# A gated cross-attention block with routed experts: rows stored, next slot numbers and row quarters issued ahead of the w1 load, the w1 split ahead of the row transposes, and another order at the seam

## The chip, the cores and the metric

The kernel runs on one core of one Trainium2 chip. The metric is the device time in microseconds (us) of one execution. A core has five engines with a queue each: TensorE (PE) multiplies matrices, VectorE (DVE), ScalarE (ACT) and GpSimd (POOL) do elementwise work, SyncE (SP) starts transfers. An instruction starts when those before it on its engine have gone ahead and the semaphores it waits for have been raised.

## The reference

The input x is 16 batches of 256 tokens with 512 features, the context as large. All is float32.

```python
x = x + tanh(g_xattn) * softmax((ln(x) @ Wq) @ (ctx @ Wk).T / sqrt(512)) @ (ctx @ Wv)
n = ln(x)                                      # layer norm again
probs = softmax(n @ gate_w + gate_b, axis=1)   # over the tokens of a batch, 8 experts
vals, idx = top_k(probs, 2)
h = relu(n @ w1[e] + b1[e]); h = relu(h @ w2[e] + b2[e]); y = relu(h @ w3[e] + b3[e])
v[e] = sum of y * w_tok over all tokens that chose expert e
x = x + tanh(g_ffn) * (sum of v[e] over the two experts of a token)
```

## The kernel before

Each float32 product is done as three products of parts: an operand is split into a rounded part (`_hi`, a copy by ACT or DVE) and the rest (`_lo`, a subtraction by DVE or POOL), and PE adds hi*hi, hi*lo and lo*hi (`split_product`, L1319 to L1321).

**First part: batches.** For each of the 16 batches the attention, the second norm and the gate are computed, the two best experts of every token are found (`two_best`), PE ranks them (`ranks`), and DVE gives every chosen token a slot in its expert's region (`slots`). POOL writes pairs of token and weight to these slots in DRAM (`send_pairs`, `slot_pair`). The normed rows go to DRAM (`xn2_dram`).

**Second part: tiles.** The slots of an expert are cut into tiles of 352. There are 24 tiles here. For a tile, the slot numbers are loaded (`load_idx`), POOL gathers the rows with three indirect transfers (`gather`, L664), and the rows are brought into feature order. For tiles 0 to 3 PE transposes them (`row_transposes`). From tile 4 on SP stores the gathered rows to `rows_dram` (`store_rows`), loads them back as four quarters (`load_quarters`, `xq`), and DVE transposes 32x32 blocks (`transpose_blocks`, L1195). ACT and DVE split the result (`et_high`, `et_low`). Then come three layers: 48 matmuls of 352 columns each (two halves of 24), with ReLU by ACT (`relu`, L836), the `_hi` cast by DVE (`h_high`, L1190) and the `_lo` subtraction by POOL (`h_low`, L674) in two halves each between them. The weights w1, w2, w3 of the tile's expert are loaded if the expert changed (`load_w`), rounded by ACT (`split_w`, L825) and subtracted by DVE (`w_low`, L930). DVE sums the third layer's result over the tile with the tokens' weights (`weighted_sum`, L1221), and `part_done` is raised.

**The order is written out by hand, one list for each engine.** In the loop, iteration j:
- PE: layer 2 of tile j, layer 1 of tile j+1, layer 3 of tile j. Layer 1 of tile m waits for `part_done` of tile m-2, layer 3 for both halves of POOL's `h_low` of layer 2.
- ACT: w3 round of j, ReLUs of layer 2 of j, w2 round of j+1, ReLUs of layer 1 of j+1, w1 round of j+2, `et_high` of j+2. The w1 round of j+2 waits until layer 1 of j+1 is through, since there is one `w_hi` and one `w_lo` for each layer.
- DVE: w3 split of j, `h_high` of layer 2 of j, w2 split of j+1, `h_high` of layer 1 of j+1, row transposes of j+2, w1 split of j+2, `et_low` of j+2, weighted sum of j.
- POOL: `h_low` of layer 2 of j, of layer 1 of j+1, gather of j+3.
- SP: w3 and b2 of j+1, w2 and b1 of j+2, w1 of j+3, rows store of j+3, b3 and token weights of j+1, quarters of j+3, slot numbers of j+4.

A load of w1 is four transfers, a rows store two, the quarters four, the slot numbers three. SP waits in order: for the w1 load that DVE has split the w1 before; for the store and for the slot numbers that the gather has landed; for the quarters that the store has landed and that the transposes before are done; for b3 and the token weights that the tile before is summed.

**The seam** is the stretch in which the last batches and the first tiles are interleaved, on each engine a list of its own between the batch pipeline and the loop (from L1238 on DVE, from L1553 on PE, from L856 on ACT).

Of the kernel before, what the change touches and what calls it, by code (L numbers as in the profile page):

```python
# [15 lines left out]
P = 128  # L16
B, S, D, E = 16, 256, 512, 8
TOK = B * S
TOPK = 2
DC = D // P  # L20
# [72 lines left out]
def has_tile(ahead, left):  # L93

    return ahead < left


def flamingo_block(nc, x, x_t, ctx_t, g_xattn, g_ffn, wq_t, wk_t, wv, gate_w, gate_b,
# [15 lines left out]
    with ExitStack() as ctx:  # L114
# [287 lines left out]
        def _(sp):  # L402
# [140 lines left out]
            def tile(j, left):  # L543
                if has_tile(1, left):
                    load_w(2, j + 1)
                    load_b(1, j + 1)
                if has_tile(2, left):
                    load_w(1, j + 2)
                    load_b(0, j + 2)
                if has_tile(3, left):  # L550
                    load_w(0, j + 3)
                    if not isinstance(j, int):
                        store_rows(j + 3)
                if has_tile(1, left):
                    load_b(2, j + 1)
                    load_wb(j + 1)
                if has_tile(3, left) and not isinstance(j, int):
                    load_quarters(j + 3)
                if has_tile(4, left):
                    load_idx(j + 4)  # L560

            tile(0, AHEAD + 1)
            tile(1, AHEAD + 1)
# [153 lines left out]
        def _(act):  # L717
# [123 lines left out]
                relu_half(n, m, 0)  # L841
                relu_half(n, m, 1)

            def et_high(m):
                need(act, l_done[0], 2 * m)
                if not isinstance(m, int):
                    act.wait_ge(et_ready, m - BY_BLOCKS + 1)
                    act.activation(et_hi[:], et[:], ACT.Copy).then_inc(et_his, TH)
                    return
                for c, (a, n) in enumerate(CHUNKS):  # L850
                    act.wait_ge(te_done, TH * m + c + 1)
                    act.activation(et_hi[:, :, a:a + n], row_banks(m)[c][:, 0:DC * n].rearrange("p (c s) -> p c s", c=DC),
                                   ACT.Copy).then_inc(et_his, 1)
# [4 lines left out]
            v_high(B - 1)  # L858
            pt_high(B - 1)
            gt_high(B - 2)  # L860
            et_high(0)
            split_w(0, 0)
            gate_exp(B - 2)
            split_w(1, 0)
            act.wait_ge(b_in[0], 16)
            relu_half(0, 0, 0)
            norm2(B - 1)
            relu_half(0, 0, 1)
            et_high(1)
            gt_high(B - 1)  # L870
            split_w(0, 1)
# [32 lines left out]
        def _(dve):  # L904
# [276 lines left out]
                dve.wait_ge(w_his[n], m + 1)  # L1181
                low(w_lo[n][:], w_raw[n][:], w_hi[n][:], w_los[n])

            def h_high(n, m):
                need(dve, l_done[n + 1], 2 * m)
                if n == 1 and isinstance(m, int) and m == 0:
                    dve.wait_ge(gate_done, B)
                for k in range(2):
                    dve.wait_ge(relu_done[n], DC * m + 2 * k + 2)
                    dve.tensor_copy(h_hi[n][:, 2 * k:2 * k + 2], h[:, 2 * k:2 * k + 2]).then_inc(h_his[n], 1)  # L1190

# [3 lines left out]
                dve.transpose(et[:].rearrange("p k (g b) -> p g k b", b=QB),  # L1195
                              xq[:].rearrange("p g (i k) -> p g k i", k=DC)).then_inc(et_ready, 1)

            def et_low(m):
                if not isinstance(m, int):
                    dve.wait_ge(et_his, TH * (m + 1))  # L1200
                    dve.tensor_tensor(et_lo[:], et[:], et_hi[:].bitcast(F32), ALU.subtract).then_inc(et_los, TH)
                    return
                for c, (a, n) in enumerate(CHUNKS):
                    dve.wait_ge(et_his, TH * m + c + 1)
                    low(et_lo[:, :, a:a + n], row_banks(m)[c][:, 0:DC * n].rearrange("p (c s) -> p c s", c=DC),
                        et_hi[:, :, a:a + n], et_los)

            def weighted_sum(m, last=False):

                dve.wait_ge(b_in[2], 16 * (m + 1))  # L1210
                dve.wait_ge(wb_in, 16 * (m + 1))
                dve.tensor_scalar(nb3[:], bias[2][:], -1.0, None, ALU.mult).then_inc(wsum_step, 1)
                dve.tensor_reduce(wsum[:], wb[:, :, 1], AX_X, ALU.add).then_inc(wsum_step, 1)
                dve.wait_ge(wsum_step, 2 * m + 2)
                for oc in range(DC):
                    if last:
                        dve.wait_ge(last_done, oc + 1)
                    elif oc % 2 == 0:
                        dve.wait_ge(l_done[2], 2 * m + oc // 2 + 1)
                    z = layer_banks(2, m)[oc][:, 0:TILE]  # L1220
                    dve.scalar_tensor_tensor(out=z, in0=z, scalar=nb3[:, oc:oc + 1], in1=wb[:, :, 1],  # L1221
                                             op0=ALU.max, op1=ALU.mult,
                                             accum_out=acc[:, oc:oc + 1]).then_inc(tail_small, 1)
                    dve.wait_ge(tail_small, DC * m + oc + 1)
                need(dve, v_acc, 2 * m)
                dve.scalar_tensor_tensor(out=part[:], in0=bias[2][:], scalar=wsum[:, 0:1], in1=acc[:],  # L1226
                                         op0=ALU.mult, op1=ALU.add).then_inc(part_done, 1)
                dve.wait_ge(part_done, m + 1)
                dve.tensor_tensor(v_add[:], part[:].unsqueeze(1).broadcast_to([P, E, DC]),
                                  tile_onehot[:, :, bass.ds(m, 1)].broadcast_to([P, E, DC]), ALU.mult  # L1230
                                  ).then_inc(v_acc, 1)
                dve.wait_ge(v_acc, 2 * m + 1)
                dve.tensor_tensor(v_sum[:], v_sum[:], v_add[:], ALU.add).then_inc(v_acc, 1)
# [4 lines left out]
            slots(B - 3, (B - 3) % 2)  # L1238
            v_pt_low(B - 1)
            gt_low(B - 2)  # L1240
            et_low(0)
            w_low(0, 0)
            gate_softmax(B - 2)
            attended(B - 1)
            w_low(1, 0)
            h_high(0, 0)
            two_best(B - 2)
            et_low(1)
            gt_low(B - 1)
# [8 lines left out]
            slots(B - 1, (B - 1) % 2)  # L1258
            w_low(0, 2)
            et_low(2)  # L1260
            weighted_sum(0)
            w_low(2, 1)
            h_high(1, 1)
# [2 lines left out]
            h_high(0, 2)  # L1266
            w_low(0, 3)
            et_low(3)
            weighted_sum(1)

            def tile(j, left):
# [3 lines left out]
                if has_tile(1, left):  # L1275
                    w_low(1, j + 1)
                    h_high(0, j + 1)
                if has_tile(2, left):
                    if not isinstance(j, int):
                        transpose_blocks(j + 2)  # L1280
                    w_low(0, j + 2)
                    et_low(j + 2)
                if has_tile(0, left):
                    weighted_sum(j, last=(left == 1))

            tiles = tiles_in_use(dve)
            tile_pipeline(dve, tile, tiles)
# [25 lines left out]
        def _(pe):  # L1313
# [54 lines left out]
            def values(m, c):  # L1368
# [2 lines left out]
                    pe.wait_ge(c_los, 1)  # L1371
                need(pe, x2_done, 2 * m)
                split_product(bV[c][:], cols(c_hi, c_lo, c * P, P), cols(wv_hi, wv_lo, 0, D), v_done)

            def ranks(m):

# [177 lines left out]
            scores(B - 1)  # L1554
            gate_transposes(B - 3)
            values(B - 1, 0)
            ranks(B - 3)
            values(B - 1, 1)
            pt_transposes(B - 1)
            xn2_transposes(B - 2)  # L1560
            need(pe, qa_los, 2 * B)
            row_transposes(0, range(2))
            gate_logits(B - 2)
            row_transposes(0, range(2, TH))
            p_times_v(B - 1)
            layer1_half(0, 0)
            gate_transposes(B - 2)
            layer1_half(0, 1)
# [92 lines left out]
```

## Time and profile before

| | |
|---|---|
| median of 3 runs | 954.54 us (951.21 to 954.67) |
| the profiled execution | 953.95 us |
| its span, first to last instruction | 952.2 us |
| PE busy, weight loads | 918.2 us (96%), 863.7 us (91%) |
| DVE, ACT, POOL busy | 721.6 us (76%), 419.5 us (44%), 454.7 us (48%) |
| mean granted clock of TensorE | 0.981 |

Batches take the first 300 us, the seam runs to about 415 us, the loop to 923 us, and the end adds the experts' sums to x. In the page's 40 slices PE is at 9 tenths nearly everywhere. [...] Times in the profile are counted from the first instruction.

### The profile page before, as it was taken

What the parts mean: (1) busy time and instruction counts of PE and PEld (TensorE: products, weight loads), DVE (VectorE), ACT (ScalarE), POOL (GpSimd) and SP (SyncE); (2) the same over time, 40 slices, a digit from 0 to 9 for tenths busy, and PEclk for the clock granted to TensorE, in tenths of its full rate; (3) what the DMA queues carried; (4) which work ended last, traced back from release to release, by engine and by line L of the source; (5) the groups of instructions that cost most, each with busy time, mean ns of one, the idle gap of its engine ahead of it and who ended that gap; (6) DMA issues with size and microseconds to landing.
All of it is one profiled execution on the core that took longest, in us unless ns stands there. A gap on an engine that the chain in (4) does not pass through costs nothing.

```text
span 952.2 us, 18810 instructions
## 1 busy us (share of the span) xinstructions
PE 918.2 (96%) x5746; PEld 863.7 (91%) x5746; DVE 721.6 (76%) x1379; ACT 419.5 (44%) x594; POOL 454.7 (48%) x402
## 2 busy tenths in 40 slices
PE   9999999999999979999999999999999999999985
PEld 6989888899888869899999999999999999999981
DVE  5667787887888867876877786889877777777646
ACT  5454443544433455344444444444444444444311
POOL 4225444444434566653655453655544554455213
PEclk9999999999999998999999999999999999999995
DMA  6433322233211544446656777866565555564008
GB/s 233 155 114 110 130 91 88 93 127 115 106 66 67 143 128 84 135 90 184 184 165 172 208 215 221 239 222 184 133 173 158 150 154 148 150 185 119 17 16 352
DMA packets 91924, 138.67 MB, mean 146 GB/s; under 512 B 28528, under 2 KB 56944, under 8 KB 88688
## 3 DMA queue, kind: packets, MB, share of 16 engines
q1 hardware_dynamic: 84464, 120.86, 42.8%
q0 software_dynamic: 7424, 17.38, 6.2%
q8 instruction: 18, 0.29, 0.1%
q14 instruction: 18, 0.15, 0.1%
HBM read 106.66 MB, written 31.53 MB: 145 GB/s over the span
## 4 chain that ended last, share of the span: by engine, by line
PE 65%; issue 11%; POOL 7%; DVE 6%; DMA 5%; SPq 4%; ACT 1%; POOLq 0%; DVEq 0%; ACTq 0%
PE bank L1319 20%; PE bank L1320 19%; PE bank L1321 19%; POOL h_lo L674 4%; POOL xg L664 3%; DMA rows_dram<-xg 2%; DMA xg<-xn_dram,idx 2%; DVE x_all L1309 2%; PE bank L1333 1%; PE bank L1390 1%; SPq L541 1%; PE bank L1431 1%; DMA idx<-slot_pair 1%; SPq L463 1%; PE bank L1433 1%
## 5 line engine op out<-in xcount | busy, mean ns | idle before, releaser
L674 POOL TENSOR_TENSOR h_lo<-h,h_hi 128x704 fp32r<-128x704 f32 x96 | 183.6, 1916 | 245.2 <-DVE h_hi L1190 245.2
L1319 PE MATMUL bank<-h_hi,w_hi 128*128 128x352 f32 x752 | 245.7, 327 | 7.3 <-POOL h_lo L674 4.1
L1321 PE MATMUL bank<-h_hi,w_lo 128*128 128x352 f32 x752 | 243.6, 324 | 0.0
L1320 PE MATMUL bank<-h_lo,w_hi 128*128 128x352 f32 x752 | 242.6, 323 | 0.0
L930 DVE TENSOR_TENSOR w_lo<-w_raw,w_hi 128x2048 fp32r<-128x2048 f32 x72 | 181.0, 2514 | 22.4 <-ACT w_hi L825 18.0
L836 ACT ACTIVATE h<-bank,bias 128x352 f32<-128x352 f32 x192 | 95.8, 551 | 201.0 <-PE bank L1321 170.8
L825 ACT ACTIVATE w_hi<-w_raw 128x2048 fp32r<-128x2048 f32 x72 | 137.8, 1916 | 54.6 <-PE bank L1321 46.0
L1319 PEld LDWEIGHTS bank<-h_hi,w_hi 128*128 128x128 f32 x752 | 142.1, 189 | 9.6 <-issue 9.6
L1320 PEld LDWEIGHTS bank<-h_lo,w_hi 128*128 128x128 f32 x752 | 142.1, 189 | 0.0
L1321 PEld LDWEIGHTS bank<-h_hi,w_lo 128*128 128x128 f32 x752 | 141.7, 188 | 0.0
L1319 PE MATMUL bank<-et_hi,w_hi 128*128 128x352 f32 x384 | 125.0, 326 | 4.5 <-DVE part L1226 2.6
L1190 DVE CAST h_hi<-h 128x704 fp32r<-128x704 f32 x96 | 69.1, 725 | 76.3 <-ACT h L836 76.3
L1320 PE MATMUL bank<-et_lo,w_hi 128*128 128x352 f32 x384 | 123.7, 322 | 0.0
L1321 PE MATMUL bank<-et_hi,w_lo 128*128 128x352 f32 x384 | 123.7, 322 | 0.0
L664 POOL DMA_INDIRECT xg<-xn_dram,idx x72 | 104.5, 1452 | 36.6 <-issue 16.6
L634 POOL DMA_INDIRECT slot_pair<-pair,slot_u x64 | 66.1, 1033 | 36.5 <-DVE pair L987 19.3
L1319 PEld LDWEIGHTS bank<-et_hi,w_hi 128*128 128x128 f32 x384 | 72.5, 189 | 5.5 <-issue 3.1
L1320 PEld LDWEIGHTS bank<-et_lo,w_hi 128*128 128x128 f32 x384 | 72.7, 189 | 0.0
L1321 PEld LDWEIGHTS bank<-et_hi,w_lo 128*128 128x128 f32 x384 | 72.6, 189 | 0.0
L601 POOL TENSOR_SCALAR rn<-mv 128x2 f32<-128x2 f32 x32 | 9.4, 293 | 131.1 <-DVE mv L927 131.1
L1319 PE MATMUL bank<-xt_hi,a_hi 128*128 128x256 f32 x240 | 69.1, 288 | 0.0
L1195 DVE STREAM_TRANSPOSE et<-xq 128x1408 f32<-128x1408 f32 x20 | 54.8, 2739 | 17.5 <-DMA xq<-rows_dram 17.4
(202 smaller groups left out, 1767.1 us busy)
## 6 DMA issues: line engine op xcount, KB each, us to landing
w_raw<-in_w SPq DMA_DIRECT2D x24, 1024.0 KB, 5.1
xq<-rows_dram SPq DMA_DIRECT2D x80, 176.0 KB, 4.1
w_raw<-in_w SPq DMA_DIRECT2D x48, 256.0 KB, 6.1
rows_dram<-xg SPq DMA_DIRECT2D x20, 512.0 KB, 3.1
wb<-slot_pair SPq DMA_DIRECT2D x24, 352.0 KB, 4.1
xt_raw<-in_x_t SPq DMA_DIRECT2D x16, 512.0 KB, 3.9
c_raw<-in_ctx_t SPq DMA_DIRECT2D x16, 512.0 KB, 3.3
x_all<-in_x SPq DMA_DIRECT2D x16, 512.0 KB, 4.8
```

The source lines that it names most:

```text
L634: pool.indirect_dma_start(slot_pair, bass.IndirectOffsetOnAxis(ap=slot_u[:, k, n:n + 1], axis=0), pair[:, k, n], None).then_inc(pair_sent[ ...
L664: pool.indirect_dma_start(xg[0:n, c], None, rows, bass.IndirectOffsetOnAxis(ap=idx[0:n, c, 0:1], axis=0)).then_inc(gathered, 16)
L674: pool.tensor_tensor(h_lo[n][:, 2 * k:2 * k + 2], h[:, 2 * k:2 * k + 2], h_hi[n][:, 2 * k:2 * k + 2].bitcast(F32), ALU.subtract).then_inc( ...
L825: act.activation(w_hi[n][:], w_raw[n][:], ACT.Copy).then_inc(w_his[n], 1)
L836: act.activation(h[:, oc], layer_banks(n, m)[oc][:, 0:TILE], ACT.Relu, bias=bias[n][:, oc:oc + 1]).then_inc(relu_done[n], 1)
L930: dve.tensor_tensor(dst, src, hi.bitcast(F32), ALU.subtract).then_inc(done, 1)
L1190: dve.tensor_copy(h_hi[n][:, 2 * k:2 * k + 2], h[:, 2 * k:2 * k + 2]).then_inc(h_his[n], 1)
L1195: dve.transpose(et[:].rearrange("p k (g b) -> p g k b", b=QB), xq[:].rearrange("p g (i k) -> p g k i", k=DC)).then_inc(et_ready, 1)
L1309: dve.tensor_tensor(row, bank[n % 8][:], row, ALU.add).then_inc(res_dve, 1)
L1319: pe.matmul(out_ap, lh, rh, start=(i == 0), stop=False)
L1320: pe.matmul(out_ap, lh, rl, start=False, stop=False)
L1321: last = pe.matmul(out_ap, ll, rh, start=False, stop=(i == n - 1))
```

## The change

In the loop DVE does the w1 split of j+2 ahead of the transposes of j+2, and the two small operations of a tile's sum that need only b3 and the token weights (`weights_of`) go between the transposes and `et_low`. SP issues the rows store, the slot numbers and the quarters ahead of the w1 load, and b3 and the token weights come last. In the seam PE puts `ranks` of batch 13 into the middle of a product, does all transposes of tile 0 in one go and moves the gate logits of batch 14 behind the attention product; ACT and DVE do the w1 split of tile 0 ahead of the third chunk of its rows, ACT both ReLU halves ahead of the last norm, DVE the first `h_high` half ahead of the w2 split.

```diff
@@ SP, tile(j, left)
+                if has_tile(3, left) and not isinstance(j, int):
+                    store_rows(j + 3)
+                if has_tile(4, left):
+                    load_idx(j + 4)
                 if has_tile(3, left):
+                    if not isinstance(j, int):
+                        load_quarters(j + 3)
                     load_w(0, j + 3)
-                    if not isinstance(j, int):
-                        store_rows(j + 3)
                 if has_tile(1, left):
                     load_b(2, j + 1)
                     load_wb(j + 1)
-                if has_tile(3, left) and not isinstance(j, int):
-                    load_quarters(j + 3)
-                if has_tile(4, left):
-                    load_idx(j + 4)
@@ ACT, seam
-            et_high(0)
+            et_high(0, range(2))
             split_w(0, 0)
+            et_high(0, range(2, TH))
             gate_exp(B - 2)
             split_w(1, 0)
             act.wait_ge(b_in[0], 16)
             relu_half(0, 0, 0)
+            relu_half(0, 0, 1)
             norm2(B - 1)
-            relu_half(0, 0, 1)
@@ DVE, seam
-            et_low(0)
+            et_low(0, range(2))
             w_low(0, 0)
+            et_low(0, range(2, TH))
             gate_softmax(B - 2)
             attended(B - 1)
+            h_high(0, 0, range(1))
             w_low(1, 0)
-            h_high(0, 0)
+            h_high(0, 0, range(1, 2))
@@ DVE, tile(j, left)
                 if has_tile(2, left):
+                    w_low(0, j + 2)
                     if not isinstance(j, int):
                         transpose_blocks(j + 2)
-                    w_low(0, j + 2)
+                    weights_of(j)
                     et_low(j + 2)
-                if has_tile(0, left):
-                    weighted_sum(j, last=(left == 1))
+                else:
+                    weights_of(j)
+                weighted_sum(j, last=(left == 1))
@@ PE, seam
             values(B - 1, 0)
-            ranks(B - 3)
-            values(B - 1, 1)
+            values_with_ranks(B - 1, 1, B - 3)    # ranks after half of the product
             pt_transposes(B - 1)
             xn2_transposes(B - 2)
             need(pe, qa_los, 2 * B)
-            row_transposes(0, range(2))
+            row_transposes(0)
+            p_times_v(B - 1)
             gate_logits(B - 2)
-            row_transposes(0, range(2, TH))
-            p_times_v(B - 1)
             layer1_half(0, 0)
```

## Rows read from the trace of the kernel before

**Rows 1.** Windows: busy time of each engine (x instructions), clock, DMA share, GB/s.
```profile
740.00:840.00 100.00, 100.00 (x626) 100.00 (x625) 76.90 (x95) 47.81 (x52) 52.07 (x32) 1.00 0.58 155
```

**Rows 2.** Waits from 425 to 905 us: us in total, times, longest.
```profile
DVE et L1195 <- DMA xq<-rows_dram: 17.4, 7, 5.0
...
PE bank L1319 <- POOL h_lo L674: 4.1, 4, 1.4
```

**Rows 3.** Timeline of PE: start, us, instruction, [idle before it, what ended it].
```profile
456.55 0.43 PE L1319 MATMUL bank<-h_hi,w_hi 128*128 128x352 f32 x1 [1.39 <-POOL h_lo L674]
...
599.34 0.42 PE L1319 MATMUL bank<-h_hi,w_hi 128*128 128x352 f32 x1 [1.38 <-POOL h_lo L674]
...
900.33 0.32 PE L1319 MATMUL bank<-h_hi,w_hi 128*128 128x352 f32 x1
```

**Rows 4.** Timeline of DVE, a tile in which nothing is late.
```profile
809.77 2.75 DVE L1195 STREAM_TRANSPOSE et<-xq 128x1408 f32<-128x1408 f32 x1
...
814.60 1.62 DVE L1201 TENSOR_TENSOR et_lo<-et,et_hi 128x1408 fp32r<-128x1408 f32 x1
...
816.85 0.59 DVE L1221 SCALAR_TENSOR_TENSOR bank<-bank,nb,wb 128x352 f32<-128x352 f32 x1
...
826.56 2.85 DVE L930 TENSOR_TENSOR w_lo<-w_raw,w_hi 128x2048 fp32r<-128x2048 f32 x1 [1.09 <-ACT w_hi L825]
...
832.83 2.76 DVE L1195 STREAM_TRANSPOSE et<-xq 128x1408 f32<-128x1408 f32 x1
```

**Rows 5.** Timeline of ACT, the same tile.
```profile
809.18 1.92 ACT L825 ACTIVATE w_hi<-w_raw 128x2048 fp32r<-128x2048 f32 x1
812.61 1.39 ACT L848 ACTIVATE et_hi<-et 128x1408 fp32r<-128x1408 f32 x1 [1.51 <-DVE et L1195]
```

**Rows 6.** Timeline of POOL, the same tile.
```profile
809.93 1.72 POOL L674 TENSOR_TENSOR h_lo<-h,h_hi 128x704 fp32r<-128x704 f32 x1 [1.36 <-DVE h_hi L1190]
...
825.55 1.71 POOL L674 TENSOR_TENSOR h_lo<-h,h_hi 128x704 fp32r<-128x704 f32 x1 [0.46 <-DVE h_hi L1190]
```

**Rows 7.** Timeline of POOL, a tile in which the quarters came late.
```profile
593.50 5.60 POOL L674 TENSOR_TENSOR h_lo<-h,h_hi 128x704 fp32r<-128x704 f32 x2 [7.89 <-DVE h_hi L1190]
...
601.74 1.70 POOL L674 TENSOR_TENSOR h_lo<-h,h_hi 128x704 fp32r<-128x704 f32 x1 [0.46 <-DVE h_hi L1190]
...
616.89 5.65 POOL L674 TENSOR_TENSOR h_lo<-h,h_hi 128x704 fp32r<-128x704 f32 x2 [6.34 <-DVE h_hi L1190]
```

**Rows 8.** Timeline of DVE, the same tile.
```profile
603.33 2.71 DVE L1195 STREAM_TRANSPOSE et<-xq 128x1408 f32<-128x1408 f32 x1 [1.67 <-DMA xq<-rows_dram]
...
610.37 0.59 DVE L1221 SCALAR_TENSOR_TENSOR bank<-bank,nb,wb 128x352 f32<-128x352 f32 x1
```

**Rows 9.** Timeline of SP's transfers, a tile with a w1 load.
```profile
816.24 2.92 SPq L463 DMA_DIRECT2D w_raw<-in_w  x4
821.15 0.40 SPq L531 DMA_DIRECT2D rows_dram<-xg  x1
...
826.69 1.86 SPq L541 DMA_DIRECT2D xq<-rows_dram  x4
```

**Rows 10.** What reads and writes w_raw, 816 to 820 us: issue to landing.
```profile
DMA to landing us min/median/max: 5.3/5.9/6.4
```

**Rows 11.** Timeline of PE in the seam.
```profile
341.87 0.43 PE L1319 MATMUL bank<-et_hi,w_hi 128*128 128x352 f32 x1 [1.93 <-DVE w_lo L930]
...
353.99 1.09 PE L1333 MATMUL bank<-ident,xn 128*128 128x128 f32 x8 [0.80 <-ACT xn L779]
357.68 0.20 PE L1379 MATMUL bank<-ind,tri_half 128*128 128x16 bf16 x1 [2.59 <-DVE ind L1053]
```

**Rows 12.** Windows of PE alone: layer 1 of tile 0, first half.
```profile
341.87:347.45 5.58, 5.58 (x24) 0.69 0.18 59
```

**Rows 13.** Timeline of DVE in the seam.
```profile
339.52 2.29 DVE L930 TENSOR_TENSOR w_lo<-w_raw,w_hi 128x2048 fp32r<-128x2048 f32 x1 [1.25 <-ACT w_hi L825]
```

**Rows 14.** Timeline of POOL in the seam.
```profile
348.44 2.43 POOL L601 TENSOR_SCALAR rn<-mv 128x2 f32<-128x2 f32 x1 [0.69 <-DVE mv L927]
```

More of the change, by code:

```diff
@@ L842, in relu, with et_high @@
                 relu_half(n, m, 1)
-            def et_high(m):
+            def et_high(m, chunks=range(TH)):
                 need(act, l_done[0], 2 * m)
@@ L849, in et_high @@
                     return
-                for c, (a, n) in enumerate(CHUNKS):
+                for c in chunks:
+                    a, n = CHUNKS[c]
                     act.wait_ge(te_done, TH * m + c + 1)
@@ L1182, in w_low, with h_high @@
                 low(w_lo[n][:], w_raw[n][:], w_hi[n][:], w_los[n])
-            def h_high(n, m):
+            def h_high(n, m, halves=range(2)):
                 need(dve, l_done[n + 1], 2 * m)
@@ L1187, in h_high @@
                     dve.wait_ge(gate_done, B)
-                for k in range(2):
+                for k in halves:
                     dve.wait_ge(relu_done[n], DC * m + 2 * k + 2)
@@ L1196, in transpose_blocks, with et_low @@
                               xq[:].rearrange("p g (i k) -> p g k i", k=DC)).then_inc(et_ready, 1)
-            def et_low(m):
+            def et_low(m, chunks=range(TH)):
                 if not isinstance(m, int):
@@ L1202, in et_low @@
                     return
-                for c, (a, n) in enumerate(CHUNKS):
+                for c in chunks:
+                    a, n = CHUNKS[c]
                     dve.wait_ge(et_his, TH * m + c + 1)
@@ L1206, in et_low, with weights_of @@
                         et_hi[:, :, a:a + n], et_los)
-            def weighted_sum(m, last=False):
+            def weights_of(m):
                 dve.wait_ge(b_in[2], 16 * (m + 1))
@@ L1213, in weighted_sum @@
                 dve.tensor_reduce(wsum[:], wb[:, :, 1], AX_X, ALU.add).then_inc(wsum_step, 1)
+            def weighted_sum(m, last=False):
                 dve.wait_ge(wsum_step, 2 * m + 2)
@@ L1260, in _ @@
             et_low(2)
+            weights_of(0)
             weighted_sum(0)
@@ L1268, in _ @@
             et_low(3)
+            weights_of(1)
             weighted_sum(1)
@@ L1373, in values, with values_with_ranks @@
                 split_product(bV[c][:], cols(c_hi, c_lo, c * P, P), cols(wv_hi, wv_lo, 0, D), v_done)
+            def values_with_ranks(m, c, ranked):
+                need(pe, x2_done, 2 * m)
+                for i in range(DC):
+                    if i == DC // 2:
+                        ranks(ranked)
+                    ch, cl = c_hi[:, i, c * P:(c + 1) * P], c_lo[:, i, c * P:(c + 1) * P]
+                    pe.matmul(bV[c][:], ch, wv_hi[:, i], start=(i == 0), stop=False)
+                    pe.matmul(bV[c][:], ch, wv_lo[:, i], start=False, stop=False)
+                    last = pe.matmul(bV[c][:], cl, wv_hi[:, i], start=False, stop=(i == DC - 1))
+                last.then_inc(v_done, 1)
             def ranks(m):
```

## The prediction

> **What bounds the kernel now.** I read the windows first: in the loop PE is busy 100.00 of 100 us at full clock [rows 1], so there an edit gains only what still stalls PE. Next the waits: DVE stood still 17.4 us, 7 times, for the quarters of the rows, and PE 4.1 us for POOL's `h_lo` [rows 2]. The timelines join the two. In the late tile DVE waits 1.67 us for `xq`, starts its sum at 610.37 [rows 8], and POOL ends the layer 2 `h_lo` at 616.89 + 5.65 = 622.54 [rows 7]. Call that moment H and the start of layer 3 L. At the tile before, H is 593.50 + 5.60 = 599.10 [rows 7] and L is 599.34 [rows 3], 0.24 later. A tile in which nothing is late lasts 832.83 - 809.77 = 23.06 us [rows 4], which is 144 matmuls of 100/626 = 0.160 us: PE's own pass. From L = 456.55 to L = 900.33 [rows 3] there are 19 tiles, and they took 443.78 us, where 19 x 23.06 = 438.1. So 5.6 us are lost in stalls in this stretch, all behind late quarters. In the seam PE stalls for 1.93, 0.80 and 2.59 us [rows 11].
>
> **The loop: DVE's new order.** The gap between PE's pass and the chain of DVE, ACT and POOL that feeds it decides. Before, that chain went from H to H in 622.54 - 599.10 = 23.44 us, 1.67 of them the wait for `xq`: without it 21.8 us, below 23.06. So PE set the pace. I now lay out the same tile in the new order, with the quarters there in time.
> - The w1 split is next after `h_hi`. It needs `w_hi`, which ACT can't begin before layer 1 of the tile ahead is through and its ReLUs are done: in the calm tile `w_hi` ends at 809.18 + 1.92 = 811.10 [rows 5]. By then POOL has begun its second `h_lo` half of layer 1, at 809.93, until 811.65 [rows 6]. And these two exclude each other: the DVE split recorded at 826.56 for 2.85 us ended at 829.41 [rows 4], 2.15 us after POOL's half that ran from 825.55 to 827.26 [rows 6]. In the late tile POOL's half runs from 601.74 to 603.44 [rows 7], so the split ends at 603.44 + 2.15 = 605.59.
> - The transposes, which could start as soon as `h_hi` was done and ran beside POOL's half in the calm tile (809.77 against 809.93 [rows 4, 6]), now start behind the split: 605.59 + 2.71 [rows 8] - 0.08 of overlap = 608.2.
> - ACT's `et_hi` started 812.61 - (809.77 + 2.75) = 0.09 after the transposes and takes 1.39 [rows 4, 5]: 609.7. Before, DVE filled that time with the split's 2.3 us; now it has the two small operations. They are 816.85 - 814.60 - 1.62 = 0.63 us with the step before the sum [rows 4], and hide.
> - `et_lo`, 1.62 [rows 4], from 609.8 to 611.4, and the sum starts there. Before, without its 1.67 us of wait, it would have started at 608.7. From the start of the sum to H it is 622.54 - 610.37 = 12.17 us [rows 7, 8]. H comes at 611.4 + 12.15 = 623.55.
>
> The chain from H to H becomes 623.55 - 599.10 = 24.45 us, more than PE's 23.06. From the first loop tile on PE waits at layer 3 in every tile, 24.45 - 23.06 = 1.4 us from start to start, of which the profile will show some 1.2 as idle, since a matmul's record overlaps the next one's. It is a closed loop: POOL's `h_lo` holds up the next tile's `h_hi` and ReLUs, so nothing is caught up. 19 x 24.45 = 464.6 us against 443.8: **+20.8 us**. This includes that the 5.6 us of the old stalls go.
>
> The row shows the exclusion (2.15 us after POOL's end). [...]
>
> **The loop: SP's new order.** The rows store, the slot numbers and the quarters no longer stand behind the w1 load, b3 and the weights. In the calm tile quarters were issued at 826.69, 5.5 us after the store at 821.15 [rows 9]. They will come 1 to 2 us earlier there and more in tiles with loads. What this is worth is the 5.6 us, counted already; the slot numbers are early for POOL in any case. What it costs lies with the w1 load, which steps past nine issues and two waits (the gather, the landing of the store). It was issued at 816.24, its four issues take 2.92 us [rows 9] and a transfer lands 5.3 to 6.4 us after issue [rows 10]. Now: the store as before at about 821, and the quarters behind its landing. That took 5.5 us behind the w1 transfers [rows 9]; without them I take 3 us, an estimate. The quarters' issues are 1.9 [rows 9], reading the table takes 0.7, so w1 goes from 826.6 to 829.5, and the last piece has landed at 829 + 6.4 = 835.4. The layer 3 start of this tile is 808.09 (900.33 - 4 x 23.06). The next w1 round is due, if it isn't to hold up the split behind POOL's half, 24.45 + 3.6 us after it, at 836.1. So a w1 load in a calm tile just makes it. Where gathers land later it is 2 to 3 us late by the same sum, and each us goes into the loop's chain. Of nine w1 loads in the loop five or six lie in the crowded stretch before 620 us. I take **+4 us**, bounds 0 and 9 x 3 = 27, nearest to the calm row. b3 and the weights come some 6 us later than before and are needed only behind the transposes of the next tile: nothing. For tile 5 the slot numbers now wait for the gather ahead of the w1 load, which delays the first quarters by about 1 us; the split goes first there, in a wait of 5.0 us [rows 2], and hides it: nothing, bounds -1 and +1.
>
> **The seam.** `ranks` in the middle of a product waits no more: 0.5 us. Tile 0's split leaves its place behind the third chunk. It started at 339.52 behind `w_hi` [rows 13]. ACT's `w_hi` used to follow the third chunk, which used to follow the gate logits; now it follows the second chunk. Chunk two's rounding comes 0.5 us earlier, with `ranks`, and ends at 334.95. From there: `w_hi` 1.9 us [rows 5] to 336.85, the split 2.29 [rows 13] to 339.15, the third chunk's rest 0.55 to 339.7, layer 1 at 339.75 in place of 341.87 [rows 11]: 2.1 us. Its first half took 5.58 us at a mean clock of 0.69 [rows 12] in place of 24 x 0.16 = 3.84; whether the clock falls again after a stall of 1.7 us is open (it fell after 1.93, not after 1.39 [rows 3, 11, 12]): 0 to 1.7 us.
>
> Then comes a new wait. POOL's small norm step was held 2.43 us [rows 14] while DVE did the w2 split and then an `h_hi`. DVE now does them in the other order, both again ahead of it. All of it comes 2.1 us earlier, so the norm is there at 353.99 - 2.1 = 351.9. PE, which had come to it at 353.99 - 0.80 = 353.2 [rows 11], gains 2.1 us by the start of layer 1 and 5.58 - 3.84 = 1.7 by the clock, and is ready at 349.4, so this stall grows from 0.80 to 2.5 us. In return the 2.59 us for `ranks` [rows 11] are hidden, since DVE, freed by the earlier ReLU half, is done with them at about 351.9. POOL's second `h_lo` half, two of 1.7 us [rows 7] behind its norm steps, ends at 353.8. Layer 2 starts at about 353.9 in place of 358.15: 4.2 us. It may run at full clock where it ran low before, or not: 0 to 2.4. I take **-4.8 us**, bounds -2 and -7. What comes after shifts as it is.
>
> **Sum.** 953.95 (the profiled execution, span 952.2) - 4.8 + 20.8 + 4 = 973.95, so 974. The median of the runs is 0.6 above the profiled one, which I leave out.
>
> **Rivals.**
> - *Faster: PE keeps the pace.* The chain stays at or below 23.06, the stalls of the loop go and the seam gains: 953.95 - 4.8 - 5.6 = 943.5. For it: each stall of the loop stood behind late quarters, and a split moved into that wait (up to 5.0 us [rows 2]) costs nothing. Against it: in the calm tiles there is no such wait, and there the split must wait for ACT. The point from which it decides is 23.06 us. 12%.
> - *The split gets ahead of POOL's half* or isn't held. It would then run from `w_hi`'s end: 1.34 us less in the late tile, a chain of 23.1, close to PE's pass. 944 as above, and in the 12%. If only some tiles are held, the excess is halved: 953.95 - 4.8 + 10 = 959 or so. 5%; a balance near nothing 3%.
> - *The w1 load comes too late* in each of its nine tiles by 3 us or more, or the clock falls in every stall: PE's pass then grows by 5.58 - 3.84 = 1.74 us [rows 12] to 24.8, and 19 x 0.35 = 7 us come on top. 981 to 997. 10%. Stalls of 1.39 us passed without it.
>
> **How the numbers follow.** The forecast has 70%, with a range of its own from 966 to 981. Slower: 70 + 10 + 5 = 85%; same (within 0.5%, 4.8 us, about what a measurement of this kernel can tell) 3%; faster 12%. The range goes from 956 to 985: it holds the forecast, the halved case and half of the dear one, and leaves out the faster side.
>
> **What would show it.** Right: PE stalls of about 1.2 us at L1319 <- POOL `h_lo` in every loop tile, from transposes to transposes 24.4 us in place of 23.06, the w1 split recorded 2.5 us or longer right behind `h_hi`, no wait of DVE for `xq`, the sum's start 2.8 us later against the end of layer 1. A wait of ACT's `w_hi` for w_raw in w1 tiles shows the load. In the seam layer 1 of tile 0 starts near 339.8, with a stall for `xn` above 2 us. Wrong: tiles of 23.06 us without stalls, which would mean that the split isn't held or that some wait I took as serial isn't; then the time is near 944.

## The result and the profile after

The changed kernel takes 984.79 us (median; 981.96 to 985.38, 6 runs) where the kernel before, beside it on the same chip, takes 953.85 (949.1 to 954.67, 6 runs): a ratio of 1.033 [1.0304, 1.0355], slower. The forecast was 974 with a range of 956 to 985, so the direction and the mechanism held, and the time came out 10.8 us above the forecast. The profiled execution has a span of 983.0 us, against 952.2.

The windows come first, over the same stretch of the loop as [rows 1]: busy time and count of PE, PEld, DVE, ACT and POOL, clock, DMA share, GB/s.

```profile
740.00:840.00 100.00, 94.32 (x581) 92.93 (x580) 85.88 (x90) 42.84 (x48) 55.01 (x29) 1.00 0.48 133
```

PE runs 581 matmuls in 100 us in place of 626, at the same full clock. So in this stretch it isn't slowed, it is idle. What it waits for is in the waits from 425 to 935 us, the answer to [rows 2]: us in total, times, longest.

```profile
DVE w_lo L932 <- ACT w_hi L825: 34.4, 20, 4.7
ACT w_hi L825 <- DMA w_raw<-in_w: 24.3, 8, 4.2
DVE et_lo L1203 <- ACT et_hi L848: 22.2, 20, 1.1
PE bank L1329 <- POOL h_lo L674: 20.0, 18, 1.4
PE bank L1329 <- DVE part L1230: 13.3, 9, 3.3
...
DVE et L1197 <- DMA xq<-rows_dram: 4.2, 1, 4.2
```

The waits for the quarters have gone from 17.4 us to 4.2, and they were cheap. In their place PE waits for POOL in nearly every tile, and ACT waits 8 times for a w1 that is still on its way. `part` is the end of a tile's sum; PE waits for it at the start of a layer 1, once in the first loop tile and otherwise only in tiles with a late w1. Now PE's timeline, answering to [rows 3] (start, us, instruction, [idle before it, what ended it]): the start of layer 2 of tile 2, which ends the seam; layer 1 in the first loop tile; and four starts of layer 3, the last being the one that stood at 900.33 before.

```profile
410.73 0.42 PE L1329 MATMUL bank<-h_hi,w_hi 128*128 128x352 f32 x1 [1.07 <-issue]
...
445.04 0.40 PE L1329 MATMUL bank<-et_hi,w_hi 128*128 128x352 f32 x1 [3.28 <-DVE part L1230]
...
454.38 0.37 PE L1329 MATMUL bank<-h_hi,w_hi 128*128 128x352 f32 x1
...
758.22 0.42 PE L1329 MATMUL bank<-h_hi,w_hi 128*128 128x352 f32 x1 [1.05 <-POOL h_lo L674]
...
782.56 0.42 PE L1329 MATMUL bank<-h_hi,w_hi 128*128 128x352 f32 x1 [0.98 <-POOL h_lo L674]
...
931.29 0.42 PE L1329 MATMUL bank<-h_hi,w_hi 128*128 128x352 f32 x1 [0.79 <-POOL h_lo L674]
```

From these starts the whole difference can be laid out. The same instructions stand at 415.03 (not among the rows shown of before), 456.55 and 900.33 before.

| stretch | before | after | difference | forecast |
|---|---|---|---|---|
| up to layer 2 of tile 2 (seam) | 415.03 | 410.73 | -4.3 | -4.8 |
| from there to the first layer 3 of the loop | 41.52 | 43.65 | +2.1 | 0 |
| 19 tiles, layer 3 to layer 3 | 443.78 | 476.91 | +33.1 | +24.8 (chain 20.8, late w1 loads 4) |
| the rest of the span | 51.87 | 51.71 | -0.2 | 0 |
| sum | 952.2 | 983.0 | +30.8 | +20 |

The tile from 758.22 to 782.56 lasts 24.34 us, where the forecast gave 24.45. What makes 476.91 out of 19 such tiles is the tiles behind a w1 load: from layer 3 to layer 3 eight tiles last 25.54 to 27.48 us, all others 24.07 to 24.35. Here is such a load in the calm stretch. First DVE, then ACT and POOL:

```profile
788.52 2.29 DVE L932 TENSOR_TENSOR w_lo<-w_raw,w_hi 128x2048 fp32r<-128x2048 f32 x1 [3.65 <-ACT w_hi L825]
790.73 2.70 DVE L1197 STREAM_TRANSPOSE et<-xq 128x1408 f32<-128x1408 f32 x1
...
795.02 1.63 DVE L1203 TENSOR_TENSOR et_lo<-et,et_hi 128x1408 fp32r<-128x1408 f32 x1 [1.11 <-ACT et_hi L848]
```

```profile
786.57 1.92 ACT L825 ACTIVATE w_hi<-w_raw 128x2048 fp32r<-128x2048 f32 x1 [3.16 <-DMA w_raw<-in_w]
793.53 1.39 ACT L848 ACTIVATE et_hi<-et 128x1408 fp32r<-128x1408 f32 x1 [5.04 <-DVE et L1197]
```

```profile
784.95 1.71 POOL L674 TENSOR_TENSOR h_lo<-h,h_hi 128x704 fp32r<-128x704 f32 x1 [0.46 <-DVE h_hi L1192]
```

SP's transfers of w1 for this round, and the landing of its four pieces:

```profile
778.09 2.91 SPq L463 DMA_DIRECT2D w_raw<-in_w  x4
```

```profile
DMA to landing us min/median/max: 4.6/5.3/6.0
```

The last piece was issued at 780.4 and landed 6.0 us later, and ACT begins at 786.57. POOL's half ends at 784.95 + 1.71 = 786.66. A split that stood behind it would have ended 2.15 later [rows 4, 6], at 788.81; this one ends at 788.52 + 2.29 = 790.81, 2.0 us later. Nothing hides this: it goes straight down through transposes, `et_hi`, `et_lo` and the sum to POOL and to PE, and the tile from 782.56 to the next layer 3 at 808.93 lasts 26.37 us. Before, the transposes stood ahead of the split and would have covered it.

In the seam, PE answers to [rows 11]:

```profile
339.81 0.40 PE L1329 MATMUL bank<-et_hi,w_hi 128*128 128x352 f32 x1 [1.34 <-DVE et_lo L932]
...
353.07 1.09 PE L1343 MATMUL bank<-ident,xn 128*128 128x128 f32 x8 [3.50 <-ACT xn L779]
...
354.87 0.63 PE L1329 MATMUL bank<-h_hi,w_hi 128*128 128x352 f32 x1 [0.41 <-POOL h_lo L674]
```

and windows of PE alone answer to [rows 12]: the first half of layer 1 of tile 0, then the first ten matmuls of its layer 2.

```profile
339.81:343.65 3.84, 3.83 (x24) 1.00 0.48 147
354.87:357.65 2.78, 2.78 (x10) 0.50 0.67 196
```

POOL, to [rows 14]:

```profile
346.91 2.62 POOL L634 DMA_INDIRECT slot_pair<-pair,slot_u  x1 [0.30 <-issue]
349.61 0.33 POOL L601 TENSOR_SCALAR rn<-mv 128x2 f32<-128x2 f32 x1
```

### The profile page after: what moved, and what is told of

It reads as the page before. It is cut to its first block, busy times and chain, and to the rows that moved or that the text cites. A ratio compares the mean times of both kernels' runs of the same rounds, so it can differ in the third digit from the quotient of the medians.

```text
span 983.0 us, 18809 instructions
## 1 busy us (share of the span) xinstructions
PE 924.5 (94%) x5746; PEld 864.7 (88%) x5746; DVE 775.4 (79%) x1379; ACT 415.9 (42%) x594; POOL 480.1 (49%) x402
## 4 chain that ended last, share of the span: by engine, by line
PE 35%; issue 34%; POOL 19%; DVE 6%; DMA 3%; ACT 1%; SPq 1%; POOLq 0%; DVEq 0%; ACTq 0%
POOL h_lo L674 12%; PE bank L1329 10%; PE bank L1330 10%; PE bank L1331 10%; POOL xg L664 5%; DVE x_all L1319 2%; DMA xg<-xn_dram,idx 1%; PE bank L1343 1%; PE bank L1412 1%; PE bank L1453 1%; DMA wq_raw<-in_wq_t 1%; DVE et L1197 1%; POOL slot_pair L634 1%; DVE w_lo L932 0%; PE bank L1455 0%
## 5 line engine op out<-in xcount | busy, mean ns | idle before, releaser
L674 POOL TENSOR_TENSOR h_lo<-h,h_hi 128x704 fp32r<-128x704 f32 x96 | 214.1, 2240 | 262.1 <-DVE h_hi L1192 262.0
L932 DVE TENSOR_TENSOR w_lo<-w_raw,w_hi 128x2048 fp32r<-128x2048 f32 x72 | 210.3, 2921 | 40.7 <-ACT w_hi L825 36.2
L1329 PE MATMUL bank<-et_hi,w_hi 128*128 128x352 f32 x384 | 126.3, 329 | 14.7 <-DVE part L1230 13.3
L1192 DVE CAST h_hi<-h 128x704 fp32r<-128x704 f32 x96 | 96.5, 1025 | 28.4 <-ACT h L836 28.4
L664 POOL DMA_INDIRECT xg<-xn_dram,idx x72 | 99.9, 1388 | 27.3 <-issue 16.8
L1329 PEld LDWEIGHTS bank<-et_hi,w_hi 128*128 128x128 f32 x384 | 73.2, 191 | 17.3 <-issue 15.7
L848 ACT ACTIVATE et_hi<-et 128x1408 fp32r<-128x1408 f32 x20 | 27.7, 1385 | 118.4 <-DVE et L1197 118.4
L601 POOL TENSOR_SCALAR rn<-mv 128x2 f32<-128x2 f32 x32 | 7.3, 228 | 130.5 <-DVE mv L929 130.4
```

The lines of the kernel that those rows point to most:

```text
L664: pool.indirect_dma_start(xg[0:n, c], None, rows, bass.IndirectOffsetOnAxis(ap=idx[0:n, c, 0:1], axis=0)).then_inc(gathered, 16)
L674: pool.tensor_tensor(h_lo[n][:, 2 * k:2 * k + 2], h[:, 2 * k:2 * k + 2], h_hi[n][:, 2 * k:2 * k + 2].bitcast(F32), ALU.subtract).then_inc( ...
L932: dve.tensor_tensor(dst, src, hi.bitcast(F32), ALU.subtract).then_inc(done, 1)
L1329: pe.matmul(out_ap, lh, rh, start=(i == 0), stop=False)
```

## Experiments

The experiments ran in three groups, each on a chip of its own with the kernel before beside it. That took 956.6 us in the first group (experiments 1 to 4), 955.25 in the second (5 to 8), and 955.08 in the third (9, 10 and the repeat of 3); each ratio is against its own group. A tile's length is from layer 3 to layer 3. "First stretch" is from layer 2 of tile 2 to the first layer 3 of the loop (41.52 before, 43.65 after), "loop" the 19 tiles behind it (443.78, 476.91), both from PE's timeline as in the table above.

**1. The changed kernel with DVE's loop order of before.**

```diff
@@ DVE, tile(j, left)
-                    w_low(0, j + 2)
                     transpose_blocks(j + 2)
-                    weights_of(j)
+                    w_low(0, j + 2)
                     et_low(j + 2)
+                    weights_of(j)
```

> The changed kernel with DVE's loop order of before (transposes, w1 split, split of the rows, then the small operations and the sum); SP's new order and the seam stay. Chain theory: the chain from one layer 2 h_lo to the next falls back to about 21.8 us, PE sets the pace with 23.06 us a tile, and the early quarters take the old stalls of 5.6 us away. With the seam's 4.3 us (layer 2 of tile 2 began at 410.73 in place of 415.03) that is 953.95 - 4.3 - 5.6 = 944 us, and 1 to 3 us more where a w1 load is later than the 4 us of slack that a calm tile has: 945, 943 to 949. Rival, SP's order is what costs (the w1 load behind the quarters holds the loop up): it stays slow, above 965.

958.15 us (956.09 to 962.26), ratio 1.0026 [1.0004, 1.0049]. First stretch 45.87, loop 448.93. Eleven of the 19 tiles are at 23.03 to 23.06 again and six at 23.11 to 23.52; two last 27.86 and 28.07, in both of which `w_hi` waited over 8 us for w1. DVE's order carries most of the loss.

**2. The changed kernel with SP's loop order of before.**

```diff
@@ SP, tile(j, left)
+                load_w(0, j + 3)
                 store_rows(j + 3)
-                load_idx(j + 4)
-                load_quarters(j + 3)
-                load_w(0, j + 3)
                 load_b(2, j + 1); load_wb(j + 1)
+                load_quarters(j + 3)
+                load_idx(j + 4)
```

> The changed kernel with SP's order of before in the loop; DVE's new order and the seam stay. Chain theory: every loop tile takes 24.4 us, also those with a w1 load, since no w_hi waits for w_raw any more; 19 x 24.45 = 464.6 from layer 3 of tile 3 to layer 3 of tile 22 in place of 476.9 in the changed kernel: 984 - 12 - 2 (first loop tile) = 970 us, 967 to 974. Rival, SP's order is what costs: PE's pace of 23.06 returns and the time is 944 to 950.

967.97 us (967.16 to 969.75), ratio 1.0124 [1.0086, 1.0162]. First stretch 40.05, loop 461.74. `w_hi` no longer waits for w1 anywhere in the loop, and the first 16 tiles last 24.29 to 24.38 us, the last three 24.06 to 24.21, so this is the closed chain alone. Its rows show the held split, DVE, POOL, then PE (two starts of layer 3, 24.33 apart) and the wait from 456 to 905 us:

```profile
749.22 3.56 DVE L932 TENSOR_TENSOR w_lo<-w_raw,w_hi 128x2048 fp32r<-128x2048 f32 x1 [0.36 <-ACT w_hi L825]
```

```profile
748.94 1.69 POOL L674 TENSOR_TENSOR h_lo<-h,h_hi 128x704 fp32r<-128x704 f32 x1 [0.46 <-DVE h_hi L1192]
```

```profile
746.54 0.42 PE L1329 MATMUL bank<-h_hi,w_hi 128*128 128x352 f32 x1 [0.98 <-POOL h_lo L674]
...
770.87 0.42 PE L1329 MATMUL bank<-h_hi,w_hi 128*128 128x352 f32 x1 [0.98 <-POOL h_lo L674]
```

```profile
PE bank L1329 <- POOL h_lo L674: 17.3, 18, 1.1
```

The split is recorded 3.56 us and ends at 752.78, 2.15 after POOL's end at 750.63, as in [rows 4, 6].

**3. Both loop orders of before, only the seam new** (both diffs above).

> The changed kernel with both orders of before in the loop, so the seam's edits alone. Layer 2 of tile 2 starts at 410.7 in place of 415.0, and the loop's stalls of before stay (5.6 us): 953.95 - 4.3 = 949.6, 948 to 951. If the gain of the seam is given back in the loop (the late quarters don't move with PE), 951 to 954.

950.7 us (946.59 to 953.06), ratio 0.9942 [0.9921, 0.9963]. First stretch 41.27, loop 439.84. It was run again in the third group:

> Both loop orders of before, only the new seam, again on this chip beside the others: 950.7 us and ratio 0.994 as before, if the seam's gain of some 5 us is real; 1.000 if that gain was the chip's.

950.0 us (946.25 to 953.07, 12 runs), ratio 0.9946 [0.9925, 0.9967]. The seam's gain is real, 5 us. First stretch 41.37, loop 443.87: two profiles of one kernel differ by 4 us in the loop, by how late the quarters come, so differences of that size between single profiles aren't to be explained.

With experiment 3 as base, DVE's order alone costs 968.0 - 950.7 = 17.3 us, SP's alone 958.2 - 950.7 = 7.5, and both together 984.8 - 950.7 = 34.1. So some 9 us arise only where both are in. The 984.8 comes from another chip than the others; by the ratios (1.0124, 1.0026 and 1.033 against 0.9942) it is 17.4, 8.0 and 37.1 us, and some 12 that arise only together.

**4. Experiment 2, with POOL's second `h_lo` half of layer 1 behind the w1 split.** If POOL isn't first, the split runs free.

```diff
@@ POOL, h_low(0, j + 1, behind=True)
                 for k in range(2):
+                    if behind and k == 1:
+                        pool.wait_ge(w_los[0], m + 2)
+                        wait_alone(pool, "pool")
                     pool.wait_ge(h_his[n], 2 * m + k + 1)
```

> As the kernel with SP's order undone, and in the loop POOL's second h_lo half of layer 1 waits until DVE's w1 split of the tile is done, so the split meets no POOL instruction. It tells apart why the split is late: held by POOL's half, or waiting for ACT's w_hi. If POOL's half is what holds it (theory): the split starts when w_hi ends, 1.3 to 1.4 us earlier against the h_lo before, the chain is 23.1 us, close to PE's 23.06, each tile 23.1 to 23.4: 949.6 - 5.6 + 19 x 0.2 = 948, 944 to 953. If the wait for w_hi is what costs and POOL's half hides behind it: no change against the run before, 970. If POOL's late half now holds layer 2 or its ReLUs: above 970.

958.34 us (956.06 to 961.92), ratio 1.0025 [1.0004, 1.0047]. First stretch 40.41, loop 450.86: 10.9 us less than in experiment 2. Tiles of 23.13 to 23.50 us mix with six of 24.23 to 25.54, which stand behind waits for quarters (9.7 us, 7 times), brought late by SP's old order.

**5. The changed kernel with w1 first in SP's list**, the rest in the new order.

```diff
@@ SP, tile(j, left)
+                load_w(0, j + 3)
                 store_rows(j + 3); load_idx(j + 4); load_quarters(j + 3)
-                load_w(0, j + 3)
                 load_b(2, j + 1); load_wb(j + 1)
```

> The changed kernel, but SP issues the w1 load ahead of the rows store again; store, slot numbers and quarters stay ahead of b3 and the token weights. If the w1 load's place alone is what SP's order adds to the loss (theory), no w_hi waits for w_raw in the loop, every tile takes 24.3 us as with SP's whole order undone, and the time is that run's: 968, 966 to 970. If the early quarters or slot numbers also cost (crowded transfers), 972 and more.

969.82 us (969.52 to 970.63), ratio 1.0171 [1.0135, 1.0206]. First stretch 42.59, loop 461.77, with the first 16 tiles at 24.32 to 24.36 and the last three at 24.08 to 24.21. `w_hi` waits for w1 in no tile. This one shift takes 15 us off the changed kernel and leaves what experiment 2 has. So the place of the w1 load explains the whole of the loop's excess over the chain, 476.91 - 461.77 = 15.1 us.

**6. Experiment 5 with DVE's order of before** (the diffs of experiments 1 and 5 together).

> The same order of SP, with DVE's loop order of before. Theory: PE sets the pace, the w1 load is in time, and the quarters no longer wait behind b3 and the token weights: the stalls of 5.6 us of the seam-only kernel shrink to 2 to 4 (the first loop tile's stays), so 947 to 950 against 950.7 for the seam alone. Rival, the quarters are late for the gather and not for their place: 950.7 as the seam alone.

954.86 us (950.99 to 957.21), ratio 0.9993 [0.9966, 1.0019]. First stretch 45.90, loop 440.21. All tiles but two are at 23.06, and what the loop gains against the kernel before the first stretch loses.

**7. Experiment 1 with SP's order of before in the two tiles written out ahead of the loop.**

```diff
@@ SP, tile(j, left), j written out
+                if isinstance(j, int):
+                    load_w(0, j + 3); load_b(2, j + 1); load_wb(j + 1); load_idx(j + 4)
+                    return
```

> The changed kernel with DVE's loop order of before, and SP's order of before in its first two tiles only (those written out ahead of the loop, in which the slot numbers of tile 5 wait for gather 4 and hold up the w1 load of tile 4). With SP's new order there, the first loop tile took 30.3 us in place of 24.4. Theory: it falls back to about 24.4, and the late w1 loads of the loop (two tiles of 28 us) stay: 958.2 - 5.9 = 952.3, 951 to 954. If it stays at 958, the first tile's lateness comes from somewhere else.

951.91 us (949.85 to 953.8), ratio 0.9977 [0.9953, 1.0001]. First stretch 41.63 in place of 45.87. SP's transfers show why, first in experiment 1, then here:

```profile
418.44 1.40 SPq L490 DMA_DIRECT2D idx<-slot_pair  x3
421.35 2.91 SPq L463 DMA_DIRECT2D w_raw<-in_w  x4
...
427.77 0.39 SPq L531 DMA_DIRECT2D rows_dram<-xg  x1
428.21 0.46 SPq L532 DMA_DIRECT2D rows_dram<-xg  x1
432.37 1.85 SPq L541 DMA_DIRECT2D xq<-rows_dram  x4
```

```profile
408.42 2.91 SPq L463 DMA_DIRECT2D w_raw<-in_w  x4
...
420.87 1.50 SPq L490 DMA_DIRECT2D idx<-slot_pair  x3
423.32 0.39 SPq L531 DMA_DIRECT2D rows_dram<-xg  x1
423.76 0.46 SPq L532 DMA_DIRECT2D rows_dram<-xg  x1
427.06 1.85 SPq L541 DMA_DIRECT2D xq<-rows_dram  x4
```

The slot numbers of tile 5 wait for the gather of tile 4, and the first rows store waits for that same gather. In experiment 1 w1, b3 and the weights stand behind the slot numbers and ahead of the store, so w1 goes out only when the gather is through; here it goes out while the gather is under way. Counted from layer 2 of tile 2 (412.99 in experiment 1, 409.93 here), the slot numbers go out at 5.45 and 10.94 us, but the store at 14.78 and 13.39, the quarters at 19.38 and 17.13, and DVE's first transposes start at 25.97 and 22.23. Of the 3.7 us between the two, 1.4 are there at the store; the rest comes with its landing and that of the quarters. DVE's wait for the first quarters falls from 8.64 to 5.12 us, in experiment 1 and then here:

```profile
438.96 2.71 DVE L1197 STREAM_TRANSPOSE et<-xq 128x1408 f32<-128x1408 f32 x1 [8.64 <-DMA xq<-rows_dram]
```

```profile
432.16 2.70 DVE L1203 STREAM_TRANSPOSE et<-xq 128x1408 f32<-128x1408 f32 x1 [5.12 <-DMA xq<-rows_dram]
```

The loop stays at 448.59 us (448.93 in experiment 1), so the gain (6 us by the medians, 0.9977 against 1.0026 or 4.7 us by the ratios) is for the most part the first stretch's.

**8. Experiment 4 with w1 first in SP's list** (the diffs of experiments 4 and 5), which was to leave neither the hold nor a late load.

> The kernel in which POOL's second h_lo half of layer 1 waits for the w1 split, with the w1 load first and the quarters ahead of b3 and the weights. Without late quarters its tiles should all be like those in which DVE didn't wait for xq: 23.1 to 23.2 us from layer to layer, so PE's pace: 950 to 953, 17 us less than with POOL's half in front. [...]

957.13 us (954.39 to 965.28), ratio 1.0026 [0.9998, 1.0053]. First stretch 43.09, loop 444.02. Against experiment 5 only POOL's half has moved, and the loop loses 17.7 us, 0.93 a tile; by the medians it is 12.7. DVE, then POOL:

```profile
741.31 2.29 DVE L935 TENSOR_TENSOR w_lo<-w_raw,w_hi 128x2048 fp32r<-128x2048 f32 x1 [0.78 <-ACT w_hi L828]
```

```profile
738.43 1.72 POOL L677 TENSOR_TENSOR h_lo<-h,h_hi 128x704 fp32r<-128x704 f32 x1 [0.47 <-DVE h_hi L1195]
743.85 1.72 POOL L677 TENSOR_TENSOR h_lo<-h,h_hi 128x704 fp32r<-128x704 f32 x1 [3.70 <-DVE w_lo L935]
```

The split takes 2.29 us, starts when `w_hi` is done, and all tiles of the loop but one (24.13) fall to 23.14 to 23.60 us. So the two orders give 2.29 us here, where POOL's half waits, and an end 2.15 us behind POOL's in experiment 2, with 3.56 recorded, where the half is under way when the split starts. The 2.15 is 0.14 less than what the split takes alone; no run shows where the 0.14 comes from.

**9. Experiment 6 with the repair of experiment 7** (the diffs of 1, 5 and 7), the version that the experiments pointed to.

> DVE's loop order as before, SP's order in the loop: w1, store, slot numbers, quarters, b3 and weights; SP's order of before in the two tiles that are written out; the new seam. Theory (the quarters stall once the first loop tile is free of the early slot numbers is gone, and DVE's old chain stays under PE's pass): all loop tiles 23.06 us, the first loop tile falls from 30.55 us to about 24.7 as in the kernel with the same repair, so about 5.8 us less than 954.9, 949 us. Rival (what the quarters lose behind the old order is little, 5.6 us of stalls at most, and comes back elsewhere): no better than the seam alone, 950 to 952 us, with waits of DVE for xq still there.

951.34 us (946.54 to 952.59, 12 runs), ratio 0.9957 [0.9937, 0.9976], beside 950.0 and 0.9946 for the seam alone on the same chip. The forecast for it was 949, and the rival held. First stretch 42.31, loop 444.95. Its waits from 425 to 905 us, and those of the seam alone:

```profile
ACT w_hi L831 <- DMA w_raw<-in_w: 19.1, 6, 5.9
DVE et L1203 <- DMA xq<-rows_dram: 17.8, 7, 5.6
```

```profile
DVE et L1197 <- DMA xq<-rows_dram: 19.1, 8, 4.6
...
ACT w_hi L825 <- DMA w_raw<-in_w: 6.9, 4, 1.9
```

The quarters are awaited as long as before, and w1 longer. Once the first stretch is repaired the quarters' earlier place is worth nothing with DVE's old order.

**10. The changed kernel with the repair of experiment 7** (that diff alone).

> The changed kernel, with SP's order of before in the two tiles that are written out. Theory (the first loop tile loses 2.1 us at the transposes' and w1's wait, and late w1 loads in the loop make up the rest): the first loop tile 26 us in place of 28.2, PE's gap before its layer 3 back to about 1.3 us, the time 2 to 3 us less than 984.8: 982. Rival (the early slot numbers in those tiles push the whole crowded stretch back, so most late w1 loads of tiles 6 to 12 go with them): 975 to 978 us.

982.79 us (981.5 to 984.13), ratio 1.03 [1.0268, 1.0332]. First stretch 40.57, 3.1 us less than with the early slot numbers; loop 476.18 in place of 476.91. So what the repair does is confined to the first stretch, and the later w1 loads are late on their own account. The profile's span is only 0.8 shorter, because the seam ended at 413.93 in it and at 410.73 in the changed kernel's.

## Why the prediction came out as it did

- **What bounds the kernel, and that DVE's order makes the chain longer than PE's pass: right.** A chain of 24.45 us was forecast; experiments 2 and 5 have 24.33 in tile after tile. The stall per tile was to be 1.2 us and is 0.98. In the changed kernel PE stalls at layer 1 as well, 13.3 us in all, in the first loop tile and where w1 is late; the forecast had it wait at layer 3 alone. Over 19 tiles the chain alone gives 461.8 (experiments 2 and 5) where 464.6 was forecast.
- **The hold between split and POOL's half: right.** 2.15 us after POOL's end in the trace of experiment 2, recorded 3.56 us where it takes 2.29 alone, and experiments 4 and 8 take most of the loss away by turning the order round. The rivals in which PE keeps the pace or the split isn't held fell.
- **The late w1 loads: the term that was mis-sized, +4 forecast, 15.1 measured** (experiment 5; 12.3 if counted from the forecast's own 464.6). The mechanism was right and its due time wrong. The prediction says that the next w1 round "is due, if it isn't to hold up the split behind POOL's half, 24.45 + 3.6 us after" the start of layer 3. But the rows give: split held until 605.59, less 2.29 for the split and 1.92 for `w_hi`, is 601.38, which is 2.04 behind the layer 3 start at 599.34 [rows 3, 4, 5, 7]. It is due at 24.45 + 2.04 = 26.5, 1.6 us earlier than in the text. By the forecast's own landing at 835.4 - 808.09 = 27.3 a calm tile is thus 0.8 late, where the text had it just in time. In the trace `w_hi` began at 786.57 - 758.22 = 28.35, which is 1.97 behind the measured 24.34 + 2.04. So beside the due time the landing was 1.0 us later than forecast. The store went out 0.6 us earlier than taken, but the quarters 774.59 - 770.50 = 4.09 us behind it, with the three issues of the slot numbers (1.43 us) in between, where 3 were taken, and w1 778.09 - 776.45 = 1.64 behind the quarters' issues, where "reading the table takes 0.7". The rows, of which the first is the store:

```profile
770.50 0.39 SPq L531 DMA_DIRECT2D rows_dram<-xg  x1
...
772.91 1.43 SPq L490 DMA_DIRECT2D idx<-slot_pair  x3
774.59 1.86 SPq L541 DMA_DIRECT2D xq<-rows_dram  x4
```

The time of a table read can be seen in SP's issues before:

```profile
641.96 0.34 SPq L496 DMA_DIRECT2D wb<-slot_pair  x1
642.57 1.86 SPq L541 DMA_DIRECT2D xq<-rows_dram  x4
645.37 1.46 SPq L490 DMA_DIRECT2D idx<-slot_pair  x3
```

The quarters, which need no read, go out 642.57 - 642.30 = 0.27 us behind the issue ahead of them, the slot numbers, with one read, 645.37 - 644.43 = 0.94: about 0.7 for a read. `load_w` reads two entries, of this tile and of the one before, so an estimate from these gaps is 0.27 + 2 x 0.67 = 1.61 us, near the 1.64 measured, where the forecast counted one read. The eight tiles behind a late load carry 15.0 us over 24.34 each, 1.2 to 3.1 apiece (the longest, 27.48 us, had a `w_hi` that waited 4.2). That is well inside the bounds of 0 to 27 but nearly four times the value chosen.
- **The slot numbers in the written-out tiles: "nothing, bounds -1 and +1", measured +2.1** in the first stretch, and 3.1 between the changed kernel and experiment 10. The first quarters were to be about 1 us late, and the split, done inside the wait of 5.0 us, was to make up for it. DVE's first transposes, in the kernel before and in the changed one:

```profile
437.11 2.72 DVE L1195 STREAM_TRANSPOSE et<-xq 128x1408 f32<-128x1408 f32 x1 [4.96 <-DMA xq<-rows_dram]
```

```profile
436.12 2.69 DVE L1197 STREAM_TRANSPOSE et<-xq 128x1408 f32<-128x1408 f32 x1 [4.23 <-DMA xq<-rows_dram]
```

They start 437.11 - 415.03 = 22.08 and 436.12 - 410.73 = 25.39 us behind layer 2 of tile 2, so 3.3 us later. The split in the wait did shorten what follows: from the transposes to layer 3 it is 18.26 us in place of 19.44, 1.2 less, and 3.3 - 1.2 = 2.1 is left. Counted was only the wait for the gather, not that w1's four issues, b3 and the weights stand behind it in the queue, and the first rows store behind those.
- **The seam: -4.8 forecast.** The changed kernel's profile has -4.3, the medians of the seam alone -5 (0.9942 and 0.9946). Layer 1 of tile 0 was forecast for 339.75 and starts at 339.81, at full clock (1.00) after a stall of 1.34. That the start fits so well is luck: in the other eleven profiles with this seam it lies between 340.22 and 343.52. The full clock is in all twelve. The stall for `xn` was to be 2.5; it is 3.50 here, 3.64 in the profile of experiment 4, and 2.53 or 2.54 in the ten others. Layer 2 starts at 354.87, not 353.9, and its first ten matmuls run at a clock of 0.50, which the prediction had left open. Single profiles place the end of this seam anywhere from 409.93 to 414.43; which part of the 5 us is whose is open.
- **The range.** It ended at 985, 0.2 above the measured median of 984.79; by the ratio, 1.033 x 954.54 = 986, it lies just outside. The dear case, 981 to 997, was given 10%; the sum with the right due time would have made it likelier.

## What to carry to other kernels

Moving work off a wait pays only in the tiles that have the wait; in the others it lengthens the chain, and a chain with 1.3 us of slack against PE loses the excess in every tile of the loop. When an instruction is pulled to the head of a chain, work out again when its inputs are due, by subtracting from the first end that really matters, and do it in writing: a load that was hidden behind another step is now on the path. And count everything that stands behind a moved wait in its queue, in the iterations that are written out as well as in the loop.

## What the hardware showed that was not expected

POOL's issues of indirect transfers, 0.91 to 1.22 us in 113 of the 136 in the changed kernel's trace, are recorded longer when they start inside one of DVE's weight splits. The one at 346.91 in the seam is recorded at 2.62 us, to 349.53, 0.84 behind the end of DVE's w2 split:

```profile
346.40 2.29 DVE L932 TENSOR_TENSOR w_lo<-w_raw,w_hi 128x2048 fp32r<-128x2048 f32 x1
```

It isn't alone. In that trace 23 issues are recorded at over 1.5 us (1.72 to 3.09). Each of them starts 0.17 to 1.75 us behind the start of a `w_lo` and ends 0.79 to 0.97 us behind its end, about the time of an issue that meets none. Eleven others overlap a `w_lo` and take 0.92 to 1.02 us; ten of them start ahead of it, one 0.01 us behind its start. The 21 that start inside a row transpose or an `h_hi` take 0.91 to 0.95 us. POOL's norm step, recorded at 2.43 us before [rows 14], takes 0.33 here and still comes late, since it now stands behind this issue.

After 1.34 us of idle time PE's clock stayed at 1.00 in the seam, after 1.93 it was 0.69 on average in the kernel before [rows 11, 12], and after 3.50 and 0.41 us, with small matmuls between, it was 0.50. In the loop stalls of 0.98 us in every tile left it at 1.00 (experiments 2 and 5). In the changed kernel's loop it fell twice, behind the stalls of 3.28 us at 445.04 and of 2.47 at 599.32, in windows of PE:

```profile
446.50:449.50 3.00, 3.00 (x12) 0.50 0.78 144
600.00:603.00 3.00, 3.00 (x13) 0.50 0.65 178
```

Neither fall moved the next layer 3, since POOL was later still: it ended its `h_lo` at 448.48 + 5.62 = 454.10 and 602.72 + 5.64 = 608.36, and layer 3 began at 454.38 and 608.66, 0.28 and 0.30 behind. So here the slow stretches of the clock cost nothing. The length of the stall alone doesn't tell whether the clock falls: 2.38 us at 444.75 in experiment 5 left it at 1.00, and 1.93 in the seam before didn't.
